# Delta-rule layer on one core: gates multiplied into the first-stage tables by GpSimd, and beta's broadcast moved

## The reference, cut to what matters

```python
q = silu(dconv_causal(x @ Wq));  k = silu(dconv_causal(x @ Wk)) * DK**-0.5;  v = silu(dconv_causal(x @ Wv))
a = sigmoid(x @ Wa + ba)                      # one decay for each head, channel and token
beta = sigmoid(x @ Wb + bb)                   # one gate for each head and token
def step(St, inp):                            # scan over the tokens
    err = einsum('bhvk,bhk->bhv', St, k_t) - v_t
    St = a_t[..., None] * St - (b_t[..., None] * err)[..., None] * k_t[:, :, None, :]
    o_t = einsum('bhvk,bhk->bhv', St, q_t)
o = layernorm(o) * ln_w + ln_b;  o = o * sigmoid(x @ Wg);  attention = o @ Wo
x = layernorm(x + attention);  x = layernorm(x + ffn(x))
```

## Time and profile before

| what | value |
|---|---|
| median of 3 runs | 2786.15 us |
| the three runs | 2783.69, 2786.15, 2802.97 us |
| the profiled execution | 2792.46 us |
| its span | 2790.7 us |
| busy: PE, DVE, ACT, POOL | 92%, 73%, 43%, 52% |
| mean granted TensorE clock | 0.968 |

### The profile page before, as it was taken

How to read it: one execution, slowest core, us unless ns; L and a number is a source line. 1 busy time by engine, 2 the same in 40 slices (tenths; PEclk the granted TensorE clock), 3 DMA queues, 4 the chain that set the end, 5 groups by cost and what they waited for, 6 DMA issues and landing times. The chain is left out here.

```text
span 2790.7 us, 50619 instructions
## 1 busy us (share of the span) xinstructions
PE 2578.7 (92%) x17812; PEld 2216.3 (79%) x17922; DVE 2042.4 (73%) x5887; ACT 1204.5 (43%) x2393; POOL 1445.2 (52%) x1216
## 2 busy tenths in 40 slices
PE   8999999999999489999999999999749997899999
PEld 6888888888888378888888888888637776788887
DVE  4776778678769279999999999989768886433333
ACT  4445445544454233333333333323568874433333
POOL 2644553455355489999889898979422220000000
PEclk9999999999999799999999999989859999999999
DMA  5466555655664855555556566555654543100000
GB/s 132 129 177 185 150 146 163 187 143 146 171 179 124 266 201 215 200 198 198 215 227 231 214 230 227 214 197 198 240 202 158 213 188 122 67 12 11 11 11 15
DMA packets 417321, 454.39 MB, mean 163 GB/s; under 512 B 122497, under 2 KB 367233, under 8 KB 393857
## 3 DMA queue, kind: packets, MB, share of 16 engines
q1 hardware_dynamic: 417152, 452.22, 48.6%
HBM read 321.49 MB, written 131.14 MB: 162 GB/s over the span
## 5 line engine op out<-in xcount | busy, mean ns | idle before, releaser
L355 PE MATMUL pa_ps<-pa_x_hi,pa_w_hi 128*128 128x512 f32 x1296 | 507.0, 391 | 9.4 <-ACT pa_y L298 5.2
L355 PE MATMUL pa_ps<-pa_x_lo,pa_w_hi 128*128 128x512 f32 x1296 | 505.1, 390 | 0.0
L355 PE MATMUL pa_ps<-pa_x_hi,pa_w_lo 128*128 128x512 f32 x1296 | 504.9, 390 | 0.0
L438 DVE SCALAR_TENSOR_TENSOR pa_cv<-pa_y,pa_taps,pa_cv 128x2048 f32<-128x2048 f32 x144 | 357.1, 2480 | 17.8
L1197 DVE TENSOR_TENSOR pb_tmp<-pb_gb,pb_ps 128x112 f32<-128x112 f32 (+6 forms) x1792 | 328.5, 221 | 25.5 <-POOL pb_gb L787 11.6
L787 POOL TENSOR_TENSOR pb_gb<-pb_gb,pb_ng 128x448 f32<-128x448 f32 (+6 forms) x448 | 331.6, 786 | 2.9 <-DMA pb_gb<-scratch_pairs 2.9
L1202 DVE TENSOR_TENSOR pb_ps<-pb_ps,pb_tmp 128x112 f32<-128x112 f32 (+6 forms) x1792 | 330.8, 226 | 0.0
L355 PEld LDWEIGHTS pa_ps<-pa_x_hi,pa_w_hi 128*128 128x128 f32 x1296 | 243.6, 188 | 67.1 <-ACT pa_y L298 9.4
L771 POOL TENSOR_TENSOR all_res<-all_res,pb_crow 128x1024 f32<-128x1024 f32 x120 | 281.9, 2367 | 6.1 <-DMA pb_crow<-scratch_crow 6.1
L355 PEld LDWEIGHTS pa_ps<-pa_x_hi,pa_w_lo 128*128 128x128 f32 x1296 | 243.7, 188 | 50.7
L355 PEld LDWEIGHTS pa_ps<-pa_x_lo,pa_w_hi 128*128 128x128 f32 x1296 | 243.6, 188 | 50.0
(11 more groups left out here) (191 smaller groups left out, 5426.9 us busy)
## 6 DMA issues: line engine op xcount, KB each, us to landing
pb_crow<-scratch_crow SPq DMA_DIRECT2D x30, 2048.0 KB, 10.0
pb_gb<-scratch_pairs SPq DMA_DIRECT2D x64, 896.0 KB, 6.6
pa_o_ng<-scratch_beta SPq DMA_DIRECT2D x16, 1024.0 KB, 7.9
scratch_ng<-pa_o_ng SPq DMA_DIRECT2D x16, 1024.0 KB, 4.5
scratch_A<-pa_o_A SPq DMA_DIRECT2D x16, 1024.0 KB, 4.5
scratch_vt<-pa_o_vt SPq DMA_DIRECT2D x16, 1024.0 KB, 4.5
scratch_q<-pa_o_q SPq DMA_DIRECT2D x16, 1024.0 KB, 6.9
scratch_g<-pa_o_g SPq DMA_DIRECT2D x16, 1024.0 KB, 7.8
```

The source lines that it names most:

```text
L355: last = nc.tensor.matmul(out, w[:, mat, k, :], xx[:, k, b * S:(b + 1) * S], start=(k == 0 and n == 0), stop=(k == KT - 1 and n == 2))
L438: nc.vector.scalar_tensor_tensor(out=out, in0=yy[:, :, k:k + S], scalar=tap(k), in1=out, op0=ALU.mult, op1=ALU.add).then_inc(s_tap, 1)
```

## The change

POOL gets twelve more products a head. After its first 17 steps, which end with the two products into `r_out[:, 0]`, it waits for DVE's `ng` and multiplies the table in `outs["vt"]` by it, in four pieces of 512 columns (so V's table carries the gates: `N_VT` = 21 steps). After `r_out[:, 1]` it makes `cg` = `ng` times the decay since the chunk's start, four pieces of 512 columns, into the buffer of `ra` (`N_CG` = 29). After `scaled_v` it makes `rg` = `ng` times the decay to the next block, four pieces of 384 columns, into `cv[0]` (`N_PR` = 33). The new tables are stored to DRAM (1 MB and 0.75 MB a head) and loaded a chunk at a time by halves in the recurrence, `cg` straight into `W`. There `start` and `cross` multiply by them where they multiplied by `rr`, and `solve` no longer multiplies by the gates; `w_of`, `ngx` and its copy on ACT go. Beta's row for head h + 1 is loaded at the end of SP's list for head h, behind the `rg` store and ahead of `g` and `k`.

```diff
@@ projections
+        outs["cg"] = ra[...]   # the buffer of ra, seen as p c b t
+        outs["rg"] = cv[0][...][:, 0:TOK * (CH - BL) // CH]
-        N_PR = 21
+        N_PR, N_VT, N_CG = 33, 21, 29
@@ sync
-            def head(h, first, left):
-                if not first:
-                    sp.wait_ge(s_st["ng"], 16 * h)
+            def load_beta(h):
                 sp.dma_start(outs["ng"][:, :, :, :].rearrange("p c b t -> p (c b t)"),
                              scr["beta"][h, :].partition_broadcast(P)).then_inc(s_bb, 16)
...
                 sp.wait_ge(s_ng, h + 1)
                 store("ng")
-                sp.wait_ge(s_pr, N_PR * (h + 1))
+                sp.wait_ge(s_pr, N_PR * h + N_CG)
                 store("A")
+                store("cg")
...
                 if left >= 2:
                     weights(h + 2)
+                sp.wait_ge(s_pr, N_PR * (h + 1))
+                store("rg")
+                if left >= 1:
+                    load_beta(h + 1)
                 sp.wait_ge(s_g, 4 * h + 8)
                 store("g")
@@ gpsimd, head
+                pool.wait_ge(s_ng, h + 1)
+                for c in range(0, NCH, 4):
+                    part = slice(CT * c, CT * (c + 4))
+                    mul(flat(tI)[:, part], flat(tI)[:, part], flat(outs["ng"])[:, part], k if c == 0 else None)
...
+                pool.wait_ge(s_pr, N_PR * h + k)
+                for c in range(0, NCH * B, 16):
+                    mul(by_block(outs["cg"])[:, c:c + 16], by_block(outs["ng"])[:, c:c + 16], scale(1)[:, c:c + 16])
+                assert n[0] == N_CG
+                pool.wait_ge(s_vt, h + 1)
+                pool.wait_ge(s_st["ng"], 16 * h + 16)
+                for c in range(0, NCH * B, 16):
+                    mul(by_block(outs["rg"])[:, c:c + 16], by_block(outs["ng"])[:, c:c + 16, 1:, :], scale(0)[:, c:c + 16, 1:, :])
@@ scalar, before the exponential
                     act.wait_ge(s_pr, N_PR * h)
+                    act.wait_ge(s_st["cg"], 16 * h)
@@ vector
             def scaled_v(h):
-                dve.wait_ge(s_pr, N_PR * (h + 1))
+                dve.wait_ge(s_pr, N_PR * h + N_VT)
...
                     if mat == V:
                         dve.wait_ge(s_zero, 3)
+                        if not first:
+                            dve.wait_ge(s_st["rg"], 16 * h)
@@ recurrence, sync
+            def load_gates(c, hf):
+                half = slice(HALF * hf, HALF * (hf + 1))
+                for name, dst in (("cg", W), ("rg", rg)):
+                    src = flat(scr[name][c, :, :, :]).rearrange("p (h t) -> p h t", h=HB)[:, half, :]
+                    sp.dma_start(flat(dst[:, half, :]), flat(src)).then_inc(s_gl[hf], 16)
@@ cycle
                 if kind != FIRST:
+                    sp.wait_ge(s_wn[1], 6 * c)
+                    load_gates(c, 1)
                     sp.wait_ge(s_x[1], solved(c - 1, 3))
                     load_gb(c, 3)
...
                 sp.wait_ge(s_m, NBL * (c + 1))
-                sp.wait_ge(s_ngx, c + 1)
-                sp.wait_ge(s_sv, scaled(c, 3, 0))
-                sp.wait_ge(s_sv, scaled(c, 1, 1))
                 load(ng[:, :, :], "ng", c + 1, s_ngl)
+                sp.wait_ge(s_wn[0], 6 * (c + 1))
+                load_gates(c + 1, 0)
...
             load_rr(0, 0)
+            for hf in range(2):
+                load_gates(0, hf)
@@ recurrence, vector, start
-                tt(w_of[hf][:, 8 * q:8 * q + 8, :], src[:, :, 0, 0:BL], rr[p][:, 1, hs, 0:1].broadcast_to([P, 8, BL]), ALU.mult)
-                tt(blocks(W[:, hs, :])[:, :, 1:, :], blocks(src[:, :, 0, :])[:, :, 1:, :], cr[:, :, 1:, :], ALU.mult)
+                tt(x_of[hf][:, 8 * q:8 * q + 8, :], src[:, :, 0, 0:BL], W[:, hs, 0:BL], ALU.mult)
+                tt(W[:, hs, BL:], src[:, :, 0, BL:], W[:, hs, BL:], ALU.mult)
@@ solve
-                ws, xs = w_of[hf], x_of[hf]
-                tt(xs, ws, gates, ALU.mult).then_inc(s_sv, 1)
+                xs = x_of[hf]
@@ cross
-                    rb = groups(rr[p][:, 0, hs, n + 1:n + 2]).broadcast_to([P, 8, 4, BL])
-                    tt(groups(w_of[hf]), src[:, :, 1, :, :], rb, ALU.mult).then_inc(s_wn[hf], 1)
+                    tt(groups(x_of[hf]), src[:, :, 1, :, :], groups(rg[:, hs, BL * n:BL * (n + 1)]), ALU.mult).then_inc(s_wn[hf], 1)
```

More of the change, by code:

```diff
@@ L118, in projections @@
         s_vt = m.sem("vt")
-        s_st = {n: m.sem(f"st_{n}") for n in ("q", "k", "ng", "vt", "A", "g", "r")}
+        s_st = {n: m.sem(f"st_{n}") for n in ("q", "k", "ng", "vt", "A", "g", "r", "rg", "cg")}
         x_rows = x.rearrange("b (s p) d -> (b s) p d", p=P)
@@ L161, in weights, with head @@
                     sp.dma_start(w_in[:, mat, :, :], w_dram[mat][:, h, :, :]).then_inc(s_w[mat], 16)
-            def head(h, first, left):
-                if not first:
-                    sp.wait_ge(s_st["ng"], 16 * h)
+            def load_beta(h):
                 sp.dma_start(outs["ng"][:, :, :, :].rearrange("p c b t -> p (c b t)"),
                              scr["beta"][h, :].partition_broadcast(P)).then_inc(s_bb, 16)
+            def head(h, first, left):
                 def store(n):
@@ L188, in head @@
                 store("k")
+            load_beta(0)
             weights(1)
@@ L206, in _ @@
             nc.gpsimd.memset(r_out[:, :, :, :, :], 0.0).then_inc(s_g, 4)
+            flat = lambda t: t[:, :, :, :].rearrange("p c b t -> p (c b t)")
+            by_block = lambda t: t[:, :, :, :].rearrange("p c b (n i) -> p (c b) n i", i=BL)
             at = lambda t, i: t[:, :, :].rearrange("p b (c n i) -> p i b c n", n=NBL, i=BL)[:, i]
@@ L255, in head @@
                     k = mul(rv[:, 1, :, :, j:j + 1], before, rv[:, 0, :, :, j:j + 1], k)
-                step(nc.gpsimd.tensor_copy(rv[:, 1, :, :, 0:1], rv[:, 0, :, :, 0:1]))
+                k = step(nc.gpsimd.tensor_copy(rv[:, 1, :, :, 0:1], rv[:, 0, :, :, 0:1]))
+                scale = lambda i: r_out[:, i, :, :, :].rearrange("p c b n -> p (c b) n").unsqueeze(3).broadcast_to([P, NCH * B, NBL, BL])
+                pool.wait_ge(s_pr, N_PR * h + k)
[6 more added lines that the diff above has]
+                    mul(by_block(outs["rg"])[:, c:c + 16], by_block(outs["ng"])[:, c:c + 16, 1:, :], scale(0)[:, c:c + 16, 1:, :])
                 assert n[0] == N_PR
@@ L513, in recurrence @@
         gb = [m.sb(f"gb{i}", [P, HB, PAIRS]) for i in range(NBL)]
-        ngx = m.sb("ngx", [P, HALF, CH // 2])
+        rg = m.sb("rg", [P, HB, CH - BL])
         tmp = m.sb("tmp", [P, HB, BL - 1])
@@ L519, in recurrence @@
         psT, psD, wx = ps[0:2], ps[2:6], ps[6:8]
-        w_of = [t[:, 0:HALF * BL].rearrange("p (h t) -> p h t", t=BL) for t in wx]
-        x_of = [t[:, HALF * BL:2 * HALF * BL].rearrange("p (h t) -> p h t", t=BL) for t in wx]
+        x_of = [t[:, 0:HALF * BL].rearrange("p (h t) -> p h t", t=BL) for t in wx]
         s_id = m.sem("id")
@@ L546, in recurrence @@
         s_sv = m.sem("sv")
-        s_ngx = m.sem("ngx")
+        s_gl = [m.sem(f"gl{i}") for i in range(2)]
         s_rs = [m.sem(f"rs{i}") for i in range(2)]
@@ L586, in recurrence @@
         turn = lambda c, n, hf: 2 * NBL * c + [[0, 2, 3, 5], [4, 6, 7, 9]][hf][n] - 1
-        scaled = lambda c, n, hf: 27 * turn(c, n, hf) + 1
         @block.sync
@@ L923, in cycle @@
                 absolutes(2)
-                act.wait_ge(s_ngl, 16 * (c + 1))
-                if kind != FIRST:
-                    act.wait_ge(s_sv, scaled(c - 1, 3, 1))
-                nc.scalar.activation(ngx[:, :, :], ng[:, HALF:HB, CH // 2:CH], ACT.Copy).then_inc(s_ngx, 1)
                 copy_x(at, past, c, 2, 0)
@@ L1179, in solve @@
                     dve.wait_ge(s_w, 2 * c + hf + 1)
-                    dve.wait_ge(s_ngl, 16 * (c + 1))
                 else:
                     dve.wait_ge(s_wn[hf], 6 * c + 2 * n)
-                gates = ng[:, HALF * hf:HALF * (hf + 1), BL * n:BL * (n + 1)]
-                if hf and n >= NBL // 2:
-                    dve.wait_ge(s_ngx, c + 1)
-                    gates = ngx[:, :, BL * n - CH // 2:BL * (n + 1) - CH // 2]
-                ws, xs = w_of[hf], x_of[hf]
-                tt(xs, ws, gates, ALU.mult).then_inc(s_sv, 1)
+                xs = x_of[hf]
                 dve.wait_ge(s_m, NBL * c + n + 1)
-                dve.wait_ge(s_sv, 27 * k + 1)
                 quarters = [(q, slice(QUART * q, QUART * (q + 1)), slice(QUART * (2 * hf + q), QUART * (2 * hf + q + 1))) for q in range(2)]
@@ L1215, in cross @@
                     dve.wait_ge(s_wv, 2 * c + hf + 1)
-                    tt(w_of[hf], w_of[hf], W[:, hs, BL * (n + 1):BL * (n + 2)], ALU.add).then_inc(s_wn[hf], 1)
+                    tt(x_of[hf], x_of[hf], W[:, hs, BL * (n + 1):BL * (n + 2)], ALU.add).then_inc(s_wn[hf], 1)
             def state(at, c, r):
@@ L1238, in cycle @@
                 solve(c, 2, 0)
+                dve.wait_ge(s_gl[1], 32 * (c + 1))
                 for j in range(4, 8):
@@ L1261, in _ @@
             dve.wait_ge(s_rl[0], 32)
```

(4 more changed lines are left out.)

10 lines of the change are left out of this document (7 added, 3 removed).

## The result

| | before | after |
|---|---|---|
| median | 2786.24 us (4 runs, 2783.69 to 2802.97) | 2931.54 us (4 runs, 2924.46 to 2938.45) |
| ratio, 95% interval | | 1.0507, 1.0466 to 1.0548 |
| profiled execution, its span | 2792.46, 2790.7 us | 2924.46, 2922.4 us |
| mean granted TensorE clock | 0.968 | 0.950 |

The account below looks back on a forecast made before the run. DVE's own round was taken to bound a head; in the recurrence PE stood at 96%. Pieces 138, beta 0, first load +3, recurrence -38: +103 us, median 2889; range 2780 to 2955, forecast's own range 2830 to 2955.

Parts of the forecast that it names:

- Twelve pieces: Projections: POOL's added products lengthen DVE's work, 0.8 us per 512 columns, 0.55 per 384: 8.6 us a head, 138 in all.
- Beta: Projections: its broadcast, moved on SP's queue, stays late, landing 3 to 17 us after POOL's first product: 0 change.
- DVE's own round sets the head: Projections: a head's 55.71 us is DVE's round, pausing only 3.40 us for ACT's exponential and 9.41 for beta.
- hidden case: Rival, projections: the 9.41 us wait for beta takes in the pieces, round stays at 55.7, time 2751 us; chance 0.12.
- First load: Before the recurrence's first turn, 1.75 MB of tables stand ahead of the decays and Gram writes: +3 us, 0 to 6.
- Recurrence: Removing the gate step takes away PE's waiting for X, 2.4 us a turn: -38 us, bounds 0 and 69.
- light pieces: Rival, projections: each piece costs 0.32 us, +26 us in all, 2812, or 2767 with beta's 2.8 us back; chance 0.13.
- full lock: Rival, projections: each piece shuts DVE out for its length, 13.2 us a head, 211 in all, 2962 us; chance 0.10.
- round that gets worse than its parts: Rival, projections: beta 10 us later every second head, or PE's clock drops; 4 us a head, 2953 us; chance 0.13.
- round of 64 us: Sign, projections: distance from one L444 group on DVE to the next is 64 us rather than 55.7.
- taps of K above 3 us: Sign, projections: DVE's convolution taps of K take 3.1 us instead of 2.35.
- waits of PE over 100 us: Sign, projections: PE's waits grow from 5 us to over 100.

Follow-up runs that it names:

- e1: The changed kernel without POOL's twelve pieces, the two new tables stored from a buffer of small numbers of equal size: 2775.7 us.
- e4: The changed kernel with all twelve pieces as memsets of the same size, each group led by a product of 4 columns: 2793.9 us.
- e11: The changed kernel with each of the twelve pieces as a copy of the same size, reading one input from SBUF: 2847.6 us.
- e6: The kernel before with beta's broadcast for the next head moved ahead of the weight loads and the g and k stores: 2777.4 us.
- e3: The changed kernel without the four rg pieces, their table stored as it lies; the vt and cg pieces stay: 2913.0 us.
- e7: The changed kernel with each of the twelve pieces cut in two (256 columns for vt and cg, 192 for rg): 2969.5 us.

## Why the prediction was right in kind, and where its terms were off

The sign and the mechanism held: POOL's products and DVE exclude one another, and the head pays. 2931.54 us lies in the range and in the forecast's own range, 42 us above its centre. That the heads' term came out so near is in part luck, as two errors in it cancel. By its steps:

- **Twelve pieces, +8.6 us a head (bounds 3.8 to 13.2).** Measured 9.06 for the heads, e1 to after 9.71. The total was near; what it is made of was not. The 8.6 us were all to be DVE's instructions made longer, and these grew by only 5.3. The price read from single taps was right for a single tap (0.81 us beside a vt piece, 0.8 taken), but not each piece meets a tap, and the mean tap is 2.83 us against 2.48 before. The other 3.7 us are waits, which the prediction put at nothing: `vt` and beta come later with a slower POOL. By groups, those of 512 columns cost the head 1.0 to 1.1 us each, not 0.8, and those of 384 cost 0.34, not 0.55.
- **Beta, 0 (bounds -2.8 to +4).** That it comes 3 to 17 us after POOL's first product, in turn, was right: 13.3 us (513.00 - 499.74) and 4.5 us (570.22 - 565.75). The wait grew all the same, from 8.8 to 11.5 us a head, so 0 was 2.7 us too low, inside the bounds. In e4, with the same transfers and cheap pieces, it is 8.9 us, and in e11, where DVE's instructions are not longer, 12.9: the growth comes from POOL being through later, not from the transfers.
- **DVE's own round sets the head.** This sentence was half true. e1 and e6 show PE's floor at 54.4 to 54.6 us, 0.65 to 0.85 under the head of before. The 9.41 us wait could in principle have taken in the pieces, as the hidden case said; it didn't, because the pieces don't run in it. They need `ng`, which needs beta.
- **First load, +3 (0 to 6).** Measured 6.5 up to the first state product, just outside.
- **Recurrence, -38.** The step that failed is "what can go is PE's waiting for X, 2.4 us a turn". That wait went almost entirely (13.9 to 3.1 us in 370), but the turn fell by 1.2 to 1.3 us, and DVE's waits for PE at the state, start and cross products grew from 4.0 to 6.6 us a turn. Measured 19.3 us between undisturbed turns, 27.9 in the two profiled executions.
- **Left out of the sum:** the two more tables to be stored behind the last head, within the edges of the stage (152.1 - 14 x 9.06 = 25 us for the first two heads, the last one and the drain); and 3.0 us behind the recurrence.
- **On the profiled executions** the forecast was 2895.5 and the result 2924.46, 29 us: 14 in the projections (152.1 against 138), 3.5 in the first load, 8 in the recurrence, 3 behind. The other 13 of the 42 us is that the profiled execution lay 6.3 us above the median before and 7.1 us below it after.

Of the rivals, hidden and light pieces fall by e1 to e3. The full lock (13.2 us a head, 2962) is too high as a sum: the wide pieces cost the head 1.0 to 1.1 us where 1.2 was its price, the narrow ones far less than 0.9, and no tap is longer by a wide piece's whole 1.15 us. The round that gets worse than its parts gave 2953 and is nearer than the forecast's 2889, by 21 us against 42. Part of it is seen: beta lands later in every second head (15.39 us of waiting, then 6.59, where 9.41 stood before), PE stands up to 6.7 us at a time, and the granted clock of the projections is 0.95 where it was 1.00. In e7 it is 0.94, in e4 1.00. What of the 9.06 us is the clock's was not measured apart and stays open; but DVE has no wait for PE in that stretch, while PE waits 81.8 us for DVE and ACT, so PE has room of its own.

The predicted signs: round of 64 us (64.31); taps of K above 3 us (9.12 / 3 = 3.04, and 8.48 / 3 = 2.83 a head later); waits of PE over 100 us (105.1 ahead of its products in the whole run); beta still several us late (15.39 and 6.59); PE's wait for X nearly gone; turn 61.8 us (62.95, wrong by half of the gain); POOL at 93% (92%).
